# Who issues the layers' weights: eight large loads move from SyncE's DMA queue to ScalarE's

## The reference, cut to what matters

```
q = ((side + b_self) @ Wq + bq), k = ((x + b_prev) @ Wk + bk), v = x @ Wv + bv     # 16 heads of 16
cond = softmax([q k_prev * s, masked by length ; q k_self * s]) @ [v ; v_self] @ Wo + bo
for l in 0, 1:
    h = shift(y);  q, k, v = split(h @ wqkv[l]);  q, k = rotary(l2norm(q) * qs, l2norm(k) * ks)
    y = y + local_attention(q, k, v) @ wo[l]                                        # 8 heads of 64
    h = layernorm(shift(y)) * g + b;  a, g = split(h @ w1[l] + b1[l])
    y = y + (a * gelu(g)) @ w2[l] + b2[l]                                           # hidden width 682
out = x + y
```

## Time and profile before

| | |
|---|---|
| median of 3 runs | 3763.35 us (3762.83 to 3767.95) |
| profiled execution | 3767.51 us, of which the span of its instructions is 3765.3 us |
| PE busy | 3602.7 us, 96% of the span |
| DVE, ACT, POOL busy | 2670.4 us (71%), 2242.3 us (60%), 788.4 us (21%) |
| DMA, mean over the span | 26 GB/s; 144 GB/s in the first of 40 slices |
| chain that ended last | PE 85%, DVE 7%, issue 3%, ACT 3%, SP's queue 1% |
| PE busy in the first four of 40 slices, in tenths | 5, 7, 8, 9 |

### The profile page before, as it was taken

How to read it: one execution, slowest core, us unless ns; L and a number is a source line. 1 busy time by engine, 2 the same in 40 slices (tenths; PEclk the granted TensorE clock), 3 DMA queues, 4 the chain that set the end, 5 groups by cost and what they waited for, 6 DMA issues and landing times.

```text
span 3765.3 us, 58543 instructions
## 1 busy us (share of the span) xinstructions
PE 3602.7 (96%) x20454; PEld 2447.4 (65%) x20454; DVE 2670.4 (71%) x7188; ACT 2242.3 (60%) x5085; POOL 788.4 (21%) x882
## 2 busy tenths in 40 slices
PE   5789999999999999999999999999999999999987
PEld 2456666666666666666666666666666666666655
DVE  2567777777777777777777777777777777777654
ACT  1246566566566666656656656666665665666653
POOL 1122221222222122222122222212222222222110
PEclk7799999999999999999999999999999999999998
DMA  5111110111111011111101111101111110111000
GB/s 144 23 24 23 29 29 20 16 24 29 29 29 29 14 20 26 29 29 29 23 13 24 30 29 29 29 17 19 24 29 29 29 26 13 21 29 24 7 6 9
DMA packets 104608, 99.34 MB, mean 26 GB/s; under 512 B 15276, under 2 KB 103040, under 8 KB 104320
## 3 DMA queue, kind: packets, MB, share of 16 engines
q1 hardware_dynamic: 104320, 95.61, 13.8%
HBM read 35.80 MB, written 8.39 MB: 12 GB/s over the span
## 4 chain that ended last, share of the span: by engine, by line
PE 85%; DVE 7%; issue 3%; ACT 3%; SPq 1%; POOL 0%; DMA 0%; DVEq 0%; ACTq 0%; POOLq 0%
PE ps L994 15%; PE ps L894 12%; PE ps L1007 9%; PE ps L908 6%; PE ps L941 5%; PE ps L961 5%; PE ps L950 4%; PE ps L809 3%; PE ps L970 3%; PE ps L928 3%; PE ps L752 3%; PE ps L762 3%; PE ps L799 3%; PE ps L781 2%; PE ps L834 2%
## 5 line engine op out<-in xcount | busy, mean ns | idle before, releaser
L559 POOL TENSOR_TENSOR inv<-ssq_f,minus_half 128x16 f32<-128x16 f32 x128 | 419.8, 3279 | 1043.9 <-DVE ssq_f L1209 1040.4
L994 PE MATMUL ps<-feed_area,w_s 128*128 128x256 f32 x2560 | 600.7, 382 | 7.3 <-DVE feed_area L1273 6.3
L994 PEld LDWEIGHTS ps<-feed_area,w_s 128*128 128x128 f32 x2560 | 480.5, 191 | 123.2 <-issue 54.1
L657 ACT ACTIVATE attn_area<-attn_area,f_nb,inv 128x128 f32<-128x128 f32 (+1 forms) x1024 | 546.3, 536 | 13.2 <-DVE f_nb L1237 11.6
L1146 DVE TENSOR_REDUCE c_mx<-ps 128x2 f32<-128x512 f32 x512 | 343.2, 687 | 180.5 <-PE ps L781 179.7
L679 ACT ACTIVATE feed_area<-ps,b_s 128x256 f32<-128x256 f32 x320 | 151.0, 473 | 386.3 <-PE ps L994 384.8
L1007 PE MATMUL ps<-feed_area,w_s 128*128 128x256 f32 x1536 | 355.2, 381 | 5.2 <-DVE feed_area L1283 1.5
L610 ACT ACTIVATE cond_area<-ps 128x512 f32<-128x512 f32 x512 | 294.9, 593 | 104.3 <-PE ps L799 103.4
L1233 DVE CUSTOM_DVE_ANT_0 attn_area<-ps,cst 128x128 f32<-128x128 f32 (+1 forms) x1024 | 303.8, 353 | 72.7 <-issue 71.2
L1007 PEld LDWEIGHTS ps<-feed_area,w_s 128*128 128x128 f32 x1536 | 281.7, 190 | 48.9 <-DVE feed_area L1283 14.6
L1283 DVE SCALAR_TENSOR_TENSOR feed_area<-ps,b_s,feed_area 128x256 f32<-128x256 f32 (+1 forms) x384 | 183.8, 479 | 169.0 <-ACT feed_area L679 166.3
(11 more groups left out here) (156 smaller groups left out, 6528.4 us busy)
## 6 DMA issues: line engine op xcount, KB each, us to landing
cond_area<-cond_area SPq DMA_DIRECT2D x384, 128.0 KB, 4.2
x_rows<-in_x SPq DMA_DIRECT2D x32, 256.0 KB, 2.8
f_rows<-in_fside_BxSxS SPq DMA_DIRECT2D x32, 256.0 KB, 3.2
res_rows<-in_x SPq DMA_DIRECT2D x32, 256.0 KB, 2.8
out<-res_rows SPq DMA_DIRECT2D x32, 256.0 KB, 2.1
wqkv_s<-in_L_ffn_wqkv SPq DMA_DIRECT2D x2, 1536.0 KB
w_s<-in_L_ffn_w SPq DMA_DIRECT2D x2, 1364.0 KB
cond_area<-cond_area SPq DMA_DIRECT2D x128, 6.0 KB
```

What stands on the lines that cost most here:

```text
L559: nc.gpsimd.tensor_tensor(inv[:, l, t, :], ssq_f[:, l, t, :], minus_half[:, :], ALU.pow).then_inc(SL[l]["inv_norm"], 1)
L657: nc.scalar.activation(soft[:, h % SOFT, lo:hi], soft[:, h % SOFT, lo:hi], ACT.Exp, bias=f_nb[:, l, q, h:h + 1], scale=inv[:, l, q, h:h + ...
L994: last = mm(ps[:, N0 + f % 2, c * N:(c + 1) * N], w1_s[:, l, k, lo:lo + P], hn[:, k, :], start=(k == 0), stop=(k == KD - 1))
```

## The change: what it does

The eight large loads leave SP's stream and stand at the head of ACT's. There they are issued in the same order as before, layer 0 and then layer 1, after a new wait for cond_loaded and before ACT's wait for setup_done. They count on the same semaphore, layers_loaded, whose total is the same. Nothing else differs: the small loads stay with SP, in their order.

```diff
             load(turns, consts[:, C_COS:C_COLS], layers_loaded)
             for l in range(DEPTH):
-                load(wqkv_s[:, l], wqkv[l].rearrange("(k p) n -> p k n", p=P), layers_loaded)
-                load(wo_s[:, l], wo[l].rearrange("(k p) n -> p k n", p=P), layers_loaded)
-                load(w1_s[:, l], w1[l].rearrange("(k p) n -> p k n", p=P), layers_loaded)
-                load(w2_s[:, l, 0:HFULL], w2[l, 0:HFULL * P].rearrange("(k p) n -> p k n", p=P), layers_loaded)
                 load(w2_s[0:HREST, l, HFULL], w2[l, HFULL * P:HID], layers_loaded)
...
         @block.scalar
         def _(act):
+            def load(dst, src):
+                act.dma_start(dst, src.rearrange("(k p) n -> p k n", p=P)).then_inc(layers_loaded, 16)
+
+            act.wait_ge(cond_loaded, 16 * COND_LOADS)
+            for l in range(DEPTH):
+                load(wqkv_s[:, l], wqkv[l])
+                load(wo_s[:, l], wo[l])
+                load(w1_s[:, l], w1[l])
+                load(w2_s[:, l, 0:HFULL], w2[l, 0:HFULL * P])
             act.wait_ge(setup_done, 1)
```

## The result

| | before | after |
|---|---|---|
| median of 22 runs each | 3766.89 us | 3759.99 us |
| lowest and highest | 3762.83, 3768.91 | 3752.95, 3764.37 |
| profiled execution, and its span | 3767.51, 3765.3 us | 3758.67, 3756.5 us |

The ratio is 0.9982, with a 95% interval of 0.9975 to 0.9988: the change makes the kernel 6.9 us faster by the medians (4.5 to 9.4 by the interval), where 6.5 was forecast. The absolute forecast, 3756.9, is 3.1 us low, because the kernel before has its median at 3766.89 over 22 runs and not at the 3763.35 of the first three.

What follows compares the result with a forecast made beforehand. PE's wait for the first placings, held by SP's issue order and full DMA engines, was the bound. Closed holes (3.9 us) plus the shadow (2.8), taken as 6.5, turn 3763.35 into 3756.9 us; range 3749.5 to 3765.5.

Steps and rivals of the forecast that it cites:

- The bound: PE's 19.5 us wait for placed operands, held by SP's issue order, shrinks to about 13; first score at about 52.
- ACT's issues: Eight large loads at ACT's head, some blocked: ACT free at 24 to 25, table load still about 24.7, no loss.
- the rival's price: ACT held in its issues until X puts the first score at X + 23.0, slower from X = 35.4; chance 0.10.
- SP's issues: SP without eight issues: small loads end at 28 to 34, placings begin at 31 to 36 in place of 41.4.
- The shadow: Five of the first twelve placings move while weights still move, half of their 5.6 us for free: 2.8 us.
- The holes: DMA engines' underused stretches at 24.5 to 27.5 and 38.5 to 42 us close: 3.9 us gained.
- The lower start: With no weights in the way, first score 16.6 us after the key's high part, at 47.7: gain 10.7 us.
- The clock: PE's granted clock during 88 matmuls after the first score: taken as 0, could bring 6.5 us or take 0.7.
- A: First sequence's placings overtake the weights entirely, as in the second sequence: gain 10.7, 3752.7 us; chance 0.17.
- B: DMA transfers are the bound and only idle stretches close: gain 3.9, 3759.5 us, or 1.4, 3762.0 us; chance 0.25.
- C: ACT is held in its load issues until 37, first score at 60.0, 1.6 us later: 3765.0 us; chance 0.10.
- D: All 88 PE matmuls run at the high clock, 6.5 us more on top of the forecast: 3750.4 us; chance 0.03.

## Why the prediction was right, point by point

- *The bound.* The wait, its place and its cause were as told: it shrank from 19.5 to 12.2 us ("about 13"), the first score came at 52.46 ("about 52", "50 to 54"), and it brought 5.9 us in the profiles. The two kernels with PE kept busy give 5.45 by the first score and 5.84 by the medians. The median difference of the change itself, 6.9, is within the noise of that. That the sum came so close is in part luck, as the next points show: two of its terms were off or failed, and what came in their place made it up.
- *ACT's issues.* Free at 25.77 where 24 to 25 was expected, and the table load 1.2 us late, hidden since SP issued the placings only from 36.91. The spacing of the blocked issues, read off SP's queue before, carried over to ACT's: by 25.77, 3.65 MB of the weights had moved, where about 3.7 was expected. They took longer than forecast because they began at 13.02 and the engines were not full in between. In the run with all loads on ACT even the rival's price came true.
- *SP's issues.* The mechanism was named, the turns between 4-byte elements and weights, but not its weight: the small loads ended at 31.6, the next rows stood behind them until 36.2, and the placings began at 36.91, later than "31 to 36". One element passed per weight packet of up to 5 KB; without the small loads ahead the placings were issued 7.4 us earlier.
- *The shadow.* This is the step that failed, though its size came out in the profiled pair, by luck. The prediction had five placings move while weights move, half for free, 2.8 us, although its own row had the engines at a share of 1.15 with placings alone. When the placings were issued, some 0.6 MB of weights were left, and the next rows stood ahead of them in SP's queue, so hardly any placing moved beside weights; and where placings did run beside weights, in the runs with the small loads later and with layer 1 later, they lost rate, down to a third. What came in its place is less busy time, with placings that moved faster after the weights had gone: 2.7 us in the profiled pair, and 48 x 0.93 - 43 x 1.00 = 1.6 in the pair with PE kept busy (10 to 58 us and 10 to 53). Its cause stays open; all that the runs show is that the order of the placings can be worth 0.9 to 1.9 us.
- *The holes.* 3.9 us expected by a sum over two stretches. Both closed, but smaller ones opened from 10 to 22 us while the loads ran, which the prediction didn't have: 3.2 or 2.5 us net, by the count used, and 3.8 (5.45 - 1.6) in the pair with PE kept busy.
- *The lower start.* The floor from the second sequence, 16.6 us from the key's high part, was right to half a us: 47.7 expected, 47.45 twice and 47.18 measured.
- *The clock.* Taken at 0 with both ends kept. The profiled pair shows 3.05 us in the changed kernel's favour; with the clock alike in the two busy kernels the stretch is the same to 0.01 us. The 88 matmuls took 15.21 us, as before.
- *The rivals.* A (the floor reached) needed the small loads and half the weights out of the way. B was nearest to what bound the changed kernel: the run with the rows later moved the first score by 1.7 us, nearer to what the rows' transfer takes (1.3) than to the 2.7 by which the issues moved. C happens when ACT gets all loads, D not at all.

## What to carry to other kernels

A load that moves to a second issuing engine no longer stands ahead of what the first one issues, and the idle stretches of the transfer engines close; but the sum of transfers stays, so look at their share first, and expect the holes' worth. Two queues take turns by packet, not by byte: small elements or small packets beside large ones get a small share, so for the earliest start what is urgent should have no bulk beside it at all (first score at 47.45 where it was 52.46, though in the kernel's time the runs can't tell the two apart). Count how many loads an issuing engine can have out before it is held (four here went freely, the rest waited), and put the others where it waits anyway.

## What the runs showed of the hardware that was not expected

- Nearly equal packet counts of the two queues while both had work (155 and 153, 387 and 387, 193 and 194, 90 and 93), also at packets of 4 bytes against 5 KB.
- The rate of the same twelve placings is not fixed: 0.20 to 0.25 MB in 2 us in the old order, 0.27 to 0.28 in the spread one, 0.30 to 0.34 in the old one when weights went before, and then up to 0.42 in the spread one. Why is open.
- Keeping PE busy through its wait holds the granted clock at 1.00 until a few us after the wait, and then the same half-busy chain runs at 0.50 (1.2 GHz) up to 120 us. In the kernels without it the clock rises for some us in between (80 to 88 us in the changed one). So nothing was gained.
